# Plain attention of a two-branch block: three places for the stacked rows of half of the heads, loops over batches written out, turned maxima in the PSUM ring, clearing and W1 in parts

## The reference

```python
xn = _layernorm(x)                      # 8 x 512 x 256
q = (src @ Wq + bq).reshape(B, T, 16, 16)   # src is xn; Wk, bk and Wv, bv alike
scores = jnp.einsum('bqhd,bkhd->bhqk', q, k) * 16 ** -0.5
probs = jax.nn.softmax(scores, axis=-1)
attn = jnp.einsum('bhqk,bkhd->bqhd', probs, v).reshape(B, T, 256)
x = _layer_norm(src + attn @ Wo + bo, ln1_g, ln1_b)
# then each row goes through W1[e], relu, W2[e] of the expert that its key names
```

## Time and profile before

| what | value |
|---|---|
| runs | 2158.83 us median of 3 (2158.79 to 2159.38) |
| profiled execution | 2159.92 us, its span 2158.1 us |
| instructions | 35151 |
| PE busy (matmul) | 1818.1 us, 84% of the span |
| DVE busy | 1284.6 us, 60% |
| POOL busy | 982.0 us, 46% |
| ACT busy | 834.5 us, 39% |
| chain that ended last | PE 36%, issue 7%, POOL 3%, DVE 3% |
| mean granted TensorE clock | 0.916 of full |

### The profile page before, as it was taken

The page is one execution under the profiler, slowest core; times in us unless marked ns, Lnnn a source line. Parts: engine busy times, 40 slices in busy tenths (PEclk is TensorE's granted clock), DMA queues, the critical chain, the costliest instruction groups (busy, mean ns, idle before and its releaser), DMA issues.

```text
span 2158.1 us, 35151 instructions
## 1 busy us (share of the span) xinstructions
PE 1818.1 (84%) x11505; PEld 1072.7 (50%) x11506; DVE 1284.6 (60%) x2862; ACT 834.5 (39%) x1144; POOL 982.0 (46%) x624
## 2 busy tenths in 40 slices
PE   4877789789788603999948999999999999999998
PEld 1323334334233303999934464655546555564654
DVE  3564666666656442777766576665657656566661
ACT  1344355454444411444413425153342424425152
POOL 3212332323322553445443738557374763738454
PEclk8688899898889956999968999999999999999999
DMA  4553322412422253565440010000101001010000
GB/s 79 146 91 123 42 39 43 55 39 29 62 36 30 98 195 109 200 230 206 152 97 11 1 40 2 11 31 1 41 2 40 2 11 31 1 40 1 10 21 11
DMA packets 72147, 130.04 MB, mean 60 GB/s; under 512 B 11047, under 2 KB 50119, under 8 KB 66125
## 3 DMA queue, kind: packets, MB, share of 16 engines
q1 hardware_dynamic: 68940, 119.89, 21.5%
q0 software_dynamic: 3072, 8.39, 1.2%
HBM read 76.09 MB, written 26.74 MB: 48 GB/s over the span
## 4 chain that ended last, share of the span: by engine, by line
PE 36%; issue 7%; POOL 3%; DVE 3%; ACT 1%; POOLq 0%; DMA 0%; SPq 0%; DVEq 0%; ACTq 0%
PE a_psS L703 10%; PE a_psO L717 9%; PE a_psO L740 6%; PE a_psM L677 4%; PE a_psS L665 4%; PE a_psS L649 2%; POOL a_k_tok L350 1%; PE a_psS L730 1%; ACT a_probs L468 1%; POOL a_oT L373 1%; POOL a_q_tok L350 1%; DVE a_junk L534 1%; DVE a_alibi L611 0%; DVE a_qL L524 0%; DVE a_rden L548 0%
## 5 line engine op out<-in xcount | busy, mean ns | idle before, releaser
L385 POOL TENSOR_TENSOR a_probs<-a_probs 128x1024 f32<-128x1024 f32 x144 | 340.7, 2392 | 316.5 <-PE a_psO L717 316.5
L534 DVE CUSTOM_DVE_ANT_0 a_junk<-a_psM,a_alibi 128x512 bf16<-128x512 f32 x512 | 333.8, 689 | 216.1 <-PE a_psM L677 216.1
L1277 DVE TENSOR_REDUCE f_n_tok<-f_psR 128x1 f32<-128x512 f32 x512 | 325.0, 682 | 226.0 <-PE f_psR L1414 224.9
L468 ACT ACTIVATE a_probs<-a_psS 128x1024 f32<-128x1024 f32 x256 | 248.9, 1024 | 284.6 <-PE a_psS L703 284.5
L1223 ACT ACTIVATE f_probs<-f_psS 128x1024 f32<-128x1024 f32 x256 | 247.7, 1021 | 217.1 <-PE f_psS L1435 217.0
L1414 PE MATMUL f_psR<-f_kP,f_qP 48*128 48x512 f32 x512 | 177.1, 551 | 114.3 <-DMA f_qP<-f_low 75.8
L717 PE MATMUL a_psO<-a_probs,a_v 128*32 128x512 f32 x2048 | 244.0, 597 | 0.0
L1414 PEld LDWEIGHTS f_psR<-f_kP,f_qP 48*128 48x128 f32 x512 | 69.4, 206 | 306.2 <-DVE f_n_tok L1277 133.2
L1448 PE MATMUL f_psO<-f_probs,f_v 128*32 128x512 f32 x1024 | 155.4, 682 | 0.7 <-ACT f_probs L1223 0.6
L677 PE MATMUL a_psM<-a_kH,a_qH 64*128 64x512 f32 x512 | 125.4, 485 | 34.5 <-DVE a_n_tok L534 29.0
L740 PE MATMUL a_psO<-a_wo,a_oT 128*128 128x256 f32 x512 | 132.0, 406 | 4.4 <-POOL a_oT L373 4.4
(11 more groups left out here) (190 smaller groups left out, 3511.3 us busy)
## 6 DMA issues: line engine op xcount, KB each, us to landing
w_w_high<-w_parts SPq DMA_DIRECT2D x19, 1024.0 KB, 5.3
w_w_low<-w_parts SPq DMA_DIRECT2D x19, 1024.0 KB, 7.3
f_kP<-f_high SPq DMA_DIRECT2D x64, 128.0 KB, 4.6
f_qP<-f_high SPq DMA_DIRECT2D x64, 128.0 KB, 6.2
sorted_x<-f_zeros SPq DMA_DIRECT2D x1, 4864.0 KB, 21.7
e_xs<-sorted_x SPq DMA_DIRECT2D x19, 256.0 KB, 2.7
sorted_z<-e_z SPq DMA_DIRECT2D x19, 256.0 KB, 2.2
f_xn<-in_L_attn_x SPq DMA_DIRECT2D x8, 512.0 KB, 4.1
```

The source lines that it names most:

```text
L385: nc.gpsimd.tensor_tensor(slots, slots, probs[:, first - GRP:first - GRP + 2, :], ALU.add).then_inc(added.sem, 1)
L468: nc.scalar.activation(probs[:, slots, :], psS[:, 2 * p:2 * p + 2, :], ACT.Exp).then_inc(exp_done.sem, 1)
L534: nc.vector.tensor_tensor_reduce(out=junk[:, a, :], in0=psM[:, a, :], in1=alibi[:, h, :], scale=1.0, scalar=-3.0e38, op0=ALU.add, op1=ALU.max,
L1277: nc.vector.tensor_reduce(n_tok[:, c, column:column + 1], psR[:, ring_bank("max", u), :], AX.X, ALU.max, negate=True).then_inc(max_done.se ...
```

## The change

There are now three half-tiles instead of two: half g of batch b lies in place (2b + g) mod 3, and `move_sides` waits only for the scores of the half three before. SP's list is written anew. The transposed maxima become items of the `psR` ring, ahead of the other extras of their period. All loops over batches are written out. Clearing is cut in eight parts, W1's loads and stores go with batches 0, 2, 4 and 6, the splits with batches 1, 3, 5 and 7. At the start TensorE and ACT wait for three transfers only, and the memsets of `kP` and `qP`, now 128x6144, stand behind the first norm's power.

```diff
     EXTRAS = {(0, 1): [("v", 1)], (0, 2): [("out", 0), ("out", 1)], (0, 3): [("out", 2), ("out", 3)],
-              (1, 0): [("proj", 0)], (1, 1): [("proj", 1)], (1, 2): [("proj", 2)], (1, 3): [("proj", 3)],
-              (3, 3): [("v", 0)]}
-    TURNED = {(0, 2): [("maxima", 1, 0)], (0, 3): [("rows", 0, 0), ("rows", 1, 2)], (1, 2): [("maxima", 2, 0)],
-              (2, 2): [("maxima", 3, 0)], (3, 2): [("maxima", 0, 0)]}
+              (1, 0): [("proj", 0)], (1, 1): [("proj", 1)], (1, 2): [("maxima", 2), ("proj", 2)],
+              (1, 3): [("proj", 3)], (2, 2): [("maxima", 3)], (3, 2): [("maxima", 0)], (3, 3): [("v", 0)]}
+    EXTRAS[0, 2] = [("maxima", 1)] + EXTRAS[0, 2]
+    TURNED = {(0, 3): [("rows", 0, 0), ("rows", 1, 2)]}
+    FILL = -(-(TILES * TOK // P) // B)
+    def place_of(b, pair):
+        return (2 * b + pair // HP) % 3 * HP + pair % HP
...
-        kP = sb("kP", [P, PAIRS, S], F32R)
-        qP = sb("qP", [P, PAIRS, S], F32R)
+        kP = sb("kP", [P, 3 * HP, S], F32R)
+        qP = sb("qP", [P, 3 * HP, S], F32R)
...
             def move_sides(b, g):
-                if not (isinstance(b, int) and b == 0):
-                    sp.wait_ge(score_ps.sem, score_ps.at(b - 1, QP * (2 * g + 2) * TT - 1))
-                    sp.sem_inc(passed, 1)
+                former = divmod(2 * b + g - 3, 2)
+                if former[0] >= 0:
+                    sp.wait_ge(score_ps.sem, score_ps.at(former[0], QP * (2 * former[1] + 2) * TT - 1))
...
             move_sides(0, 0)
             load_rows(0)
+            move_sides(0, 1)
             move_maxima(0, 0)
-            move_sides(0, 1)
-            sp.dma_start(sorted_x.rearrange("(n p) d -> p n d", p=P),
-                         zeros[:, :].unsqueeze(1).to_broadcast([P, TILES * TOK // P, D])).then_inc(cleared, 16)
...
-            def batch(b, more, last):
+            for b in range(B):
+                more = b + 1 < B
                 move_maxima(b, 1)
+                if b + 2 < B:
+                    load_rows(b + 1)
+                if more:
+                    move_sides(b + 1, 0)
                 move_maxima(b, 2)
                 if more:
-                    if not last:
-                        load_rows(b + 1)
-                    move_sides(b + 1, 0)
+                    move_sides(b + 1, 1)
                 move_maxima(b, 3)
+                if b % 2 == 0:
+                    if b:
+                        store_w1(b // 2 - 1)
+                    load_w1(b // 2)
+                clear_rows(b)
                 if more:
                     move_maxima(b + 1, 0)
-                    move_sides(b + 1, 1)
...
             nc.gpsimd.memset(wo[:, :, :], 0.0).then_inc(zeroed, 1)
+            nc.gpsimd.memset(zeros[:, :], 0.0).then_inc(zeroed, 1)
+            nc.gpsimd.memset(v[:, :, :, FH:], 1.0).then_inc(zeroed, 1)
+            norm0.raise_variance(pool, 0)
             nc.gpsimd.memset(kP[:, :, :].bitcast(F32), 1.0).then_inc(zeroed, 1)
             nc.gpsimd.memset(qP[:, :, :].bitcast(F32), 0.0).then_inc(zeroed, 1)
-            norm0.raise_variance(pool, 0)
...
+                if b % 2:
+                    split_w1(b // 2)
-            batch(0, False, True, range(NE // 2))
-            with pool.Fori(1, B - 1) as b:
-                batch(b, True, True)
-            batch(B - 1, True, False, range(NE // 2, NE))
+            for b in range(B):
+                batch(b, b > 0, b + 1 < B)
```

More of the change, by code:

```diff
@@ L848, in present @@
     def present(b, kind, n):
-        batch = b + belongs(kind, n)
-        return not isinstance(batch, int) or 0 <= batch < B
+        return 0 <= b + belongs(kind, n) < B
     ring = []
@@ L959, in plain_attention_phase @@
         read = {"max": lambda n: (max_done, n), "proj": lambda n: (high_done, n), "v": lambda n: (v_done, n),
-                "out": lambda n: (r1_done, n)}
-        taken = {"maxima": n_row_done, "rows": xnT_sb}
+                "out": lambda n: (r1_done, n), "maxima": lambda n: (n_row_done, n)}
         block = ctx.enter_context(nc.Block())
@@ L1140, in _, with batch @@
             keep_rows(0, True)
-            def batch(b, before, more, splits=()):
+            def batch(b, before, more):
                 if more:
@@ L1178, in _ @@
             o_taken.grant(act)
-            act.wait_ge(loads, LOADS)
+            act.wait_ge(weights_in, WEIGHTS)
             for c in range(KC):
@@ L1230, in batch @@
                         exponentials(b, r, p)
-                    for kind, n, bank in turned_in(b, r):
-                        take(b, kind, n, bank, not before and n == 1)
+                    for kind, c, bank in turned_in(b, r):
+                        take_rows(b + 1, c, bank)
                     if j == 0:
@@ L1239, in batch @@
                             take_output(b - 1, QUADS - 1)
-                    if more:
-                        for kind, n in EXTRAS.get((quad, j), ()):
-                            if kind == "proj":
-                                take_sides(b + 1, n)
+                    for kind, n in EXTRAS.get((quad, j), ()):
+                        if kind == "proj" and more:
+                            take_sides(b + 1, n)
+                        elif kind == "maxima" and present(b, kind, n):
+                            take_maxima(b + belongs(kind, n), n)
             for c in range(KC):
-                take(-1, "rows", c, 2 * c)
+                take_rows(0, c, 2 * c)
+            act.wait_ge(loads, LOADS)
+            nc.scalar.mul(bqk[:, 1::2], bqk[:, 1::2], FH ** -0.5).then_inc(scaled, 1)
+            act.wait_ge(scaled, SCALED + 1)
             for n in range(SIDES):
                 take_sides(0, n, True)
-            take(-1, "maxima", 0, 0, True)
-            batch(0, False, True)
-            with act.Fori(1, B - 1) as b:
-                batch(b, True, True)
-            batch(B - 1, True, False)
+            take_maxima(0, 0)
+            for b in range(B):
+                batch(b, b > 0, b + 1 < B)
             take_output(B - 1, QUADS - 1)
@@ L1413, in multiply_for_max @@
                 bank_read(b, "max", u)
-                nc.tensor.matmul(psR[:, ring_bank("max", u), :], qP[half, pair, c * P:(c + 1) * P],
-                                 kP[half, pair, :], start=True, stop=True,
+                place = place_of(batch, pair)
+                nc.tensor.matmul(psR[:, ring_bank("max", u), :], qP[half, place, c * P:(c + 1) * P],
+                                 kP[half, place, :], start=True, stop=True,
                                  tile_position=(FB * a, 0)).then_inc(max_ps.sem, 1)
```

134 lines of the change are left out of this document (56 added, 78 removed).

## The result

| | before | after |
|---|---|---|
| runs | 2159.11 us median of 4 (2158.79 to 2160.63) | 2198.62 us median of 4 (2194.27 to 2201.22) |
| profiled execution | 2159.92 us, span 2158.1 us | 2201.22 us, span 2199.4 us |
| first TensorE work behind the plain attention | 769.17 us | 778.55 us |
| first projection of the rotary stage | 1113.7 us | 1124.7 us |
| from there to the end | 1044.4 us | 1074.7 us |

The ratio of the runs is 1.0191, 95% interval 1.0163 to 1.0219: slower, by 39.5 us where 6 were forecast. Single executions scatter more than these four: in later sessions the kernel before had medians of 2155.6 and 2157.0 us and took 2142 to 2171 us (one slow execution of 2268 us apart). Of the 41.3 us between the two spans 9.4 arise in the stage that was changed, 1.6 in routing and experts, and 30.3 in the rotary stage, in whose code not a line differs.

The account below looks back on a forecast made before the run. TensorE, busy 84% of the span, was taken as the bound, idling in plain attention for half-tile transfers and DVE. Terms -63.3 + 21 + 71.4 - 7.7 - 16.1 + 0 + 0.4 = +5.7 us on 2158.8 gave 2165 us, range 2114 to 2182.

Parts of the forecast that it names:

- written-out loops are **0** too: Plain attention: writing out the loops over batches, TensorE's included, was taken to cost nothing, 0 us.
- The waits that go: Plain attention, periods 10 and 2: TensorE's waits for half-tiles vanish, with the slow clock after them, -63.3 us.
- Period 8: Plain attention: scores wait 3.0 us, seven times, for quad 2's maxima queued behind half 0, +21 us.
- Period 12: Plain attention, batches 0 to 6: scores wait 9.6 us for quad 3's maxima behind half 1; +71.4 us with slow clock.
- The clock: TensorE in plain attention: one slow period per long wait, 12.2 us saved after half-tile waits, 4.2 us added at period 12.
- Batches 0 and 1: Quad 1's maxima wait in batch 0 goes, -7.7 us; output projection's wait for POOL in batch 1 goes, -16.1 us.
- The ring: Turned maxima in the ring: scores' 5.4 us waits for ACT's copy go, 6.4 us of others come; 0, from -8 to +8.
- The start: Kernel start: DVE's four operations on `xn` are held behind POOL's memsets and end by 19.1 us, +0.4 us.
- A: Rival, plain attention: maxima pass the half-tiles' transfers, period 8 does not wait, period 12 waits 5.3 us; 2114 us, chance 0.16.
- B: Rival, kernel start: DVE is not held by the memsets; 2156 us, chance 0.20.
- C: Rival: low clock lasts over two periods after 9.6 us waits, or W1's transfers reach quad 0's maxima; 2183 us, chance 0.14.
- D: Rival, plain attention: half-tiles come early and nothing comes late; 2073 us, chance 0.04.

Follow-up runs that it names:

- run with all parts: Changed kernel, maxima of quads 2 and 3 issued earlier on SP, TensorE's rotary loop written out, POOL's clearing held until batch 0 is normalised: 2064.46 us, ratio 0.9557.
- run with quad 3 first: Changed kernel with SP moving the maxima of quad 3 ahead of the next batch's half-tile 1, quad 2's still behind half-tile 0: 2130.16 us.

## Why the prediction was wrong

The sign of the forecast, slower, was right, and the time was missed by 33 us, outside the range. The step that failed is one sentence: "so written-out loops are **0** too". It looked for idle time inside the loops that were being written out. Whoever writes out a loop also moves all code behind it, and behind it was a loop of TensorE's that turns seven times. There it cost 30 us. With the loop moved clear, the kernel takes 2168 us against a forecast of 2165; against the kernel before in the same session that is 11 us more, or 14 by the ratio, where 6 were forecast. This closeness is in part luck, as the point on the clock shows. The prediction did name the sign to look for, idle time with no releaser; it had no price for it and no rival on it. The other steps:

- **The waits that go.** As worked out. No wait for half-tiles at periods 10 and 2, and DVE's waits behind them returned by only 2.3 us (33.5 to 35.8) instead of the 12 that were taken off.
- **Period 8.** Seven waits of 2.3 to 3.6 us, 21.2 us; the sum had 21. The maxima land with the half.
- **Period 12.** 67.2 us of waiting was forecast, 46.6 was measured, 4.3 to 9.6 each. The release was right: 20.8 us after period 9's scores (464.54 to 485.34), forecast 20.4. The due time was off: 13.8 us after period 9 instead of 11.0 (10.8 by the rows that it names). In the batch shown the clock had come back after the wait in period 8 (granted 1.00 from 464.5 to 469.4 us) and then fell again, to 0.57 from 471 to 478 us. Where the waits in period 8 were taken away, the same batch kept the full clock there, period 12 was due 11.4 us after period 9, and six of the seven waits were 9.3 to 9.7 us, the forecast's 9.6.
- **The clock.** This was the mis-sized term. I had given each long wait one slow period and none to the waits of 3 us. In the changed trace the eight weighings took 1.93 us behind all seven waits of period 8, and the slow level then held for one to four periods; the parts of the sum on the clock give 13 us less busy time. It rose by 24.2 (582.4 to 606.6 us). That the stage still came out near the sum (7 or 9.7 us by the means, +9.4 in the profiled pair, 5.7 forecast) is two errors against each other: the sum has 5.7 + 13 = 19 us more idle time where it fell by 15 (9.4 - 24.2), 33 us off, and 13 us less busy time where it rose by 24, 37 us off the other way.
- **Batches 0 and 1.** Both waits are gone. The output projection's only idle time in the ring is 2.3 us, where it waited 13.14 us.
- **The ring.** The waits for ACT's copy went from 5.4 to 0.7 us.
- **The start.** DVE was held behind both memsets; TensorE began at 19.45 us, 0.8 us later (0.4 forecast). The Trainium skill ("SBUF — State Buffer", on the shared port pair), as quoted in the prediction, agrees for the first memset, which began 0.06 us before DVE's operation; the trace adds that DVE did not get in between the two. The run with all parts shows the other side: memsets behind, 1.38 us. One reading of the prediction was wrong: the operation of 4 columns was not as long as the memset beside it (3.51 us, from 5.58 to 9.09), it ended with it (6.09 to 9.11). In the changed trace, with no memset beside it, it took 0.17 us.
- **The rivals.** A: the period-12 waits and the 69.2 us rule it out. B: it takes an edit of its own, which brought the first scores 7.9 us sooner and the stage's end 4.8. C: its size for the clock was nearer than the forecast's, but its second half, W1's transfers at the maxima of quad 0, appears only once the waits of period 12 are gone. D: no.
- **What can be told apart.** The prediction took 4.3 us for the least difference that shows. Single runs of the kernel before later lay between 2142 and 2171 us, so only medians of many runs tell that little.

## What to carry to other kernels

Writing out a loop, or any edit that makes an engine's program longer, moves every loop behind it on that engine; look for idle time without a releaser a few instructions behind each later jump back, and move the loop by some empty instructions (64 were enough here) or write it out before judging the edit. On one queue, put the small transfer that is due soon ahead of, or into, the large one that is needed later. A short wait that comes in every batch can cost as much through TensorE's clock as through its own length, or more (here 22 to 38 us beside 21), so sum busy time as well as idle time when a wait is priced.

## What was not expected of the hardware

In this kernel a jump back on TensorE cost 0.7 to 1.3 us of idle time even in a good place, and where a border of the code lay some 4 to 8 matmuls behind the target, a second stall of 1.4 to 3.8 us with slow matmuls behind it; together some 5 us more for each of the six jumps, in passes of 130 us. The places tried show a stall at 0, +8 and +256 instructions and none at +64, +128 and +192, and by the traces' count none at +30 and +35 either, so it ends between 8 and 30. A bad place of the kernel before was not run; by the same count it would take 93 increments, which is an estimate from 163 and 256.

In the changed kernel a wait of 2.31 us was enough for the slow level behind it (1.93 us for eight weighings instead of 1.06), and the level was seen again 13 us later, with the full clock between. A wait of that length does not always bring it on. In the run with quad 3 first, period 8 of batch 3 kept the full clock behind a longer one (timeline of PE):

```profile
345.96 0.73 PE L1427 MATMUL f_psS<-f_qP,f_kP 64*128 64x512 f32 x4 [2.79 <-DMA f_qP<-f_n_row]
346.62 1.06 PE L1440 MATMUL f_psO<-f_probs,f_v 128*32 128x512 f32 x8
```

What tells the two cases apart was not tested. From run to run the plain stage of the kernel before differed by up to 13 us, that of the changed kernel by up to 22.
